# A transformer layer on eight cores: one program block for the first stage, a LayerNorm scaling moved from VectorE to ScalarE, and LayerNorm statistics taken block by block

## The reference, cut to what matters

```python
x = x + layernorm(attn(layernorm(x)))      # low-rank q and kv (rmsnorm inside), rope, 32 heads
x = x + layernorm(ffn(layernorm(x)))       # x @ W_base.T + b_base + top-2 of 8 rank-16 adapters
# layernorm: (x - mean) / sqrt(var + 1e-5) over 4096 columns, no weights
```

## Time and profile before

| | |
|---|---|
| median of 3 runs | 4936.53 us (4935.33 to 4947.84) |
| the profiled execution, its own time | 4936.56 us |
| its span on the slowest core (6) | 4935.0 us |
| spans of all cores | 4914.4 to 4935.0 us |
| PE busy | 3475.6 us (70%) |
| ACT busy | 1290.4 us (26%) |
| DVE busy | 981.7 us (20%) |

### The profile page before, as it was taken

How to read it: one execution, slowest core, us unless ns; L and a number is a source line. 1 busy time by engine, 2 the same in 40 slices (tenths; PEclk the granted TensorE clock), 3 DMA queues, 4 the chain that set the end, 5 groups by cost and what they waited for, 6 DMA issues and landing times. The chain is left out here.

```text
span 4935.0 us, 43733 instructions; the slowest of 8 cores (4914.4 to 4935.0 us)
## 1 busy us (share of the span) xinstructions
PE 3475.6 (70%) x16282; PEld 1368.9 (28%) x16282; DVE 981.7 (20%) x2552; ACT 1290.4 (26%) x1957; POOL 66.7 (1%) x129
## 2 busy tenths in 40 slices
PE   2444358188888888888888888879998038824881
PEld 1222234032232222223222222214443023312330
DVE  2454400511111111111111111100000630033004
ACT  0111100034444444444443444430000230013001
POOL 0000000000000000000000000000000000000000
PEclk9666679588889888888988888889999559966995
DMA  4111131110000000000000000023331326531662
GB/s 103 64 56 69 47 65 26 22 21 2 13 14 15 14 15 14 3 12 14 14 14 14 14 9 6 1 51 66 69 70 35 119 41 114 110 95 37 112 114 79
DMA packets 31375, 219.00 MB, mean 44 GB/s; under 512 B 3888, under 2 KB 4160, under 8 KB 14784
## 3 DMA queue, kind: packets, MB, share of 16 engines
q0 software_dynamic: 17776, 147.97, 16.1%
q1 hardware_dynamic: 13392, 68.24, 3.7%
HBM read 347.37 MB, written 16.78 MB: 74 GB/s over the span
## 5 line engine op out<-in xcount | busy, mean ns | idle before, releaser
L69 ACT ACTIVATE pool<-sPP,pool 128x512 bf16<-128x512 f32 x1024 | 700.0, 687 | 588.7 <-PE sPP L69 588.3
L69 PE MATMUL sPP<-pool 128*128 128x512 bf16 (+1 forms) x2048 | 781.3, 416 | 2.8 <-DVE pool L69 2.8
L69 PE MATMUL PEp<-pool 128*128 128x128 bf16 (+2 forms) x3872 | 595.8, 310 | 147.7 <-DVE pool L69 78.2
L69 PE MATMUL PDq<-pool 128*1 128x512 bf16 (+3 forms) x1792 | 504.8, 344 | 171.6 <-DVE pool L69 117.6
L69 PE MATMUL fP<-pool 128*128 128x512 bf16 (+1 forms) x2176 | 519.7, 397 | 74.7 <-DMA pool<-wbt 37.2
L69 ACT ACT_TABLE_LOAD x92 | 118.0, 1283 | 1531.7 <-PE trP L69 468.6
L69 DVE BATCH_NORM_STATS2 pool<-pool 128x6 f32<-128x512 bf16 (+1 forms) x344 | 208.4, 675 | 1464.6 <-PEq L1681 598.8
L69 PE MATMUL oP<-pool 128*128 128x512 bf16 x2048 | 458.5, 388 | 56.0 <-ACT pool L69 31.1
L69 PE MATMUL PCq<-pool 128*128 128x512 bf16 x1024 | 430.7, 421 | 0.0
L69 PEld LDWEIGHTS PEp<-pool 128*128 128x128 bf16 (+1 forms) x3872 | 301.6, 101 | 445.2 <-issue 292.2
L69 PE MATMUL trP<-pool 128*128 128x128 bf16 (+1 forms) x688 | 80.4, 300 | 417.3 <-DVE pool L69 363.1
(11 more groups left out here) (58 smaller groups left out, 1134.2 us busy)
## 6 DMA issues: line engine op xcount, KB each, us to landing
pool<-wbt POOLq DMA_DIRECT2D x64, 1024.0 KB, 8.6
pool<-xb SPq DMA_DIRECT2D x24, 2048.0 KB, 7.7
pool<-wo POOLq DMA_DIRECT2D x16, 2048.0 KB, 13.2
pool<-wqb POOLq DMA_DIRECT2D x16, 1152.0 KB, 8.9
out<-pool SPq DMA_DIRECT2D x64, 256.0 KB, 2.0
pool<-wqa POOLq DMA_DIRECT2D x4, 3072.0 KB, 21.4
pool<-wkvb POOLq DMA_DIRECT2D x16, 512.0 KB, 10.9
pool<-wkva POOLq DMA_DIRECT2D x1, 4608.0 KB, 32.0
```

The lines of the kernel that those rows point to most:

```text
L69: r = a(*args, **kw)
```

## The change

Stage A1 becomes one block. The load of a tile is issued a step earlier, ln(it) stands ahead of kvchain(it-2) on DVE, and the 4096-column scaling is an ACT instruction. In `a1_kvchain`, `v_rsqrt` gets a wait for that ACT instruction of tile i+2, which reads the shared `col_a`. In stages C and D the statistics of each column block are taken when ACT has copied it out, during the matmuls of the following blocks; `bn_aggr` and one 1/sqrt over all tiles of the stage or group at once (`v_rsqrtN`, the same 15 operations on 128x8 or 128x4) follow the last block. Seven small buffers are added to each of the two stages.

```diff
+    def v_rsqrtN(v, src_ap, out_ap, tx, tt, mg, eps):
...
     def a1_ln(blk, i):
...
-                ln_finish(v, ("ln1sq", i), par)
-                S_.wait(v, tok.get(("lnT_mm_all", i - 2)))
-                v.tensor_scalar(out=ln1_bufs[par][:], in0=x_bufs[par][:],
-                                scalar1=col_a[par][:], scalar2=col_b[par][:],
-                                op0=ALU.mult, op1=ALU.add)
-                tok[("lnapply", i)] = sigV.inc(v.last)
+                tok[("ln1fin", i)] = ln_finish(v, ("ln1sq", i), par)
...
     def a1_kvchain(blk, i):
...
                 S_.wait(v, tok[("kv_ms", i)])
+                if i + 2 < KT:
+                    S_.wait(v, tok[("lnapply", i + 2)])
                 v_rsqrt(v, par, col_c[par][:], 1e-30)
...
-    for it in range(KT + 2):
-        with nc.Block() as blk:
+    with nc.Block() as blk:
+        a1_xload(blk, 0)
+        for it in range(KT + 2):
+            if it + 1 < KT:
+                a1_xload(blk, it + 1)
             if it < KT:
-                a1_xload(blk, it)
+                a1_ln(blk, it)
             if 1 <= it <= KT:
                 a1_kvmm(blk, it - 1)
             if 2 <= it:
                 a1_kvchain(blk, it - 2)
             if it < KT:
-                a1_ln(blk, it)
                 a1_transpose(blk, it)
+
+        @blk.scalar
+        def _(s):
+            s = LastW(s)
+            for i in range(KT):
+                par = i % 2
+                S_.wait(s, tok[("ln1fin", i)])
+                S_.wait(s, tok[("xload", i)])
+                S_.wait(s, tok.get(("lnT_mm_all", i - 2)))
+                s.activation(out=ln1_bufs[par][:], in_=x_bufs[par][:],
+                             func=AF.Identity,
+                             scale=col_a[par][:], bias=col_b[par][:])
...
+                for wv in range(nwA):
+                    S_.wait(s, tok[("lnT_mm", i, wv)])
...
+                    s.copy(out=dst, in_=trP[par][:, 0:nk * 128])
...
@@ stage C, vector @@
+            for b in range(NOB):
+                for ti in range(QT):
+                    S_.wait(v, tok[("o_evac", b, ti)])
+                    v.bn_stats(out=ln3st[:, ti, 6 * b:6 * b + 6],
+                               in_=x1_sb[:, ti, b * OBW:(b + 1) * OBW])
...
+            for ti in range(QT):
+                v.bn_aggr(out=mvv3[:, ti, :], in_=ln3st[:, ti, :])
...
+            v_rsqrtN(v, mvf[:, 1:2 * QT:2], rstd8[:], rs8x[:], rs8t[:],
+                     magic8[:], LN_EPS)
...
+            tok["ln3rdy"] = sigV.inc(v.last)
             for ti in range(QT):
                 par = ti % 2
-                S_.wait(v, tok[("o_evac", NOB - 1, ti)])
-                S_.wait(v, tok.get(("ln3ap", ti - 2)))
-                ln_stats(v, x1_sb[:, ti, :], D, ("ln3s", ti), par)
-                S_.wait(v, tok[("ln3s", ti)])
-                v_rsqrt(v, par, mv[par][:, 1:2], LN_EPS)
-                tok[("ln3sq", ti)] = sigV.inc(v.last)
-                tok[("ln3fin", ti)] = ln_finish(v, ("ln3sq", ti), par)
                 S_.wait(v, tok[("ln3ap", ti)])
                 S_.wait(v, tok[("xr", ti)])
@@ stage C, scalar @@
-                S_.wait(s, tok[("ln3fin", ti)])
+                S_.wait(s, tok["ln3rdy"])
                 S_.wait(s, tok.get(("x1_done", ti - 1)))
                 s.activation(out=t1_buf[:], in_=x1_sb[:, ti, :],
```

More of the change, by code:

```diff
@@ L323, in v_rsqrt @@
                 S_.wait(v, t)
+    def v_rsqrtN(v, src_ap, out_ap, tx, tt, mg, eps):
+        v.tensor_scalar(out=tx, in0=src_ap, scalar1=float(eps),
+                        scalar2=None, op0=ALU.add)
+        t = sigV.inc(v.last)
+        S_.wait(v, t)
+        xi = tx.bitcast(mybir.dt.int32)
+        yi = out_ap.bitcast(mybir.dt.int32)
+        v.tensor_scalar(out=yi, in0=xi, scalar1=1, scalar2=None,
+                        op0=ALU.arith_shift_right)
+        t = sigV.inc(v.last)
+        S_.wait(v, t)
+        v.scalar_tensor_tensor(out=yi, in0=yi, scalar=-1.0,
+                               in1=mg.bitcast(mybir.dt.int32),
+                               op0=ALU.mult, op1=ALU.add)
+        t = sigV.inc(v.last)
+        S_.wait(v, t)
+        for it_ in range(3):
+            v.tensor_tensor(out=tt, in0=out_ap, in1=out_ap, op=ALU.mult)
+            t = sigV.inc(v.last)
+            S_.wait(v, t)
+            v.tensor_tensor(out=tt, in0=tt, in1=tx, op=ALU.mult)
+            t = sigV.inc(v.last)
+            S_.wait(v, t)
+            v.tensor_scalar(out=tt, in0=tt, scalar1=-0.5, scalar2=1.5,
+                            op0=ALU.mult, op1=ALU.add)
+            t = sigV.inc(v.last)
+            S_.wait(v, t)
+            v.tensor_tensor(out=out_ap, in0=out_ap, in1=tt, op=ALU.mult)
+            if it_ < 2:
+                t = sigV.inc(v.last)
+                S_.wait(v, t)
     def ln_stats(v, src, width, key, px):
@@ L420, in a1_transpose @@
         if True:
-            sS0 = sigS.count
             @blk.tensor
@@ L432, in _ @@
                     if wv > 0:
-                        S_.wait(t, (sigS, sS0 + wv))
+                        S_.wait(t, tok[("lnT_evac", i, wv - 1)])
                     for k in range(wv * 16, min(wv * 16 + 16, DK)):
@@ L438, in _ @@
                 tok[("lnT_mm_all", i)] = tok[("lnT_mm", i, nw - 1)]
[L440 to L455, removed]
     def a1_kvmm(blk, i):
@@ L576, in _ @@
                 tok[("kcT_evac", i)] = sigV.inc(v.last)
-    for it in range(KT + 2):
-        with nc.Block() as blk:
+    nwA = (DK + 15) // 16
+    aS0 = sigS.count
+    for i in range(KT):
+        base = aS0 + i * (nwA + 1)
+        tok[("lnapply", i)] = (sigS, base + 1)
+        for wv in range(nwA):
+            tok[("lnT_evac", i, wv)] = (sigS, base + 2 + wv)
+        tok[("lnT_done", i)] = tok[("lnT_evac", i, nwA - 1)]
+    with nc.Block() as blk:
[3 more added lines that the diff above has]
+                a1_xload(blk, it + 1)
             if it < KT:
-                a1_xload(blk, it)
+                a1_ln(blk, it)
             if 1 <= it <= KT:
@@ L586, in build_program @@
             if it < KT:
-                a1_ln(blk, it)
                 a1_transpose(blk, it)
+        @blk.scalar
+        def _(s):
+            s = LastW(s)
+            for i in range(KT):
+                par = i % 2
[5 more added lines that the diff above has]
+                             scale=col_a[par][:], bias=col_b[par][:])
+                tk = sigS.inc(s.last)
+                assert tk == tok[("lnapply", i)]
+                for wv in range(nwA):
+                    S_.wait(s, tok[("lnT_mm", i, wv)])
+                    nk = min(16, DK - wv * 16)
+                    if i < QT:
+                        dst = ln1T_own[:, i, wv * 16 * 128:(wv * 16 + nk) * 128]
+                    else:
+                        dst = ln1T_tmps[par][:, wv * 16 * 128:(wv * 16 + nk) * 128]
+                    s.copy(out=dst, in_=trP[par][:, 0:nk * 128])
+                    tk = sigS.inc(s.last)
+                    assert tk == tok[("lnT_evac", i, wv)]
     psA1.close()
@@ L1198, in build_program @@
     xr_buf = [xr_buf0, xr_buf0]
+    ln3st = calloc(128, [QT, 6 * NOB], F32)
+    mvv3 = calloc(128, [QT, 2], F32)
+    rstd8 = calloc(128, [QT], F32)
+    negmb8 = calloc(128, [QT], F32)
+    rs8x = calloc(128, [QT], F32)
+    rs8t = calloc(128, [QT], F32)
+    magic8 = calloc(128, [QT], F32)
     t1_buf = calloc(128, [D], BF16)
@@ L1244, in _ @@
             v = LastW(v)
+            v.memset(magic8[:].bitcast(mybir.dt.int32), 0x5F3759DF)
+            for b in range(NOB):
[3 more added lines that the diff above has]
+                               in_=x1_sb[:, ti, b * OBW:(b + 1) * OBW])
+            t = sigV.inc(v.last)
+            S_.wait(v, t)
+            for ti in range(QT):
+                v.bn_aggr(out=mvv3[:, ti, :], in_=ln3st[:, ti, :])
+            t = sigV.inc(v.last)
+            S_.wait(v, t)
+            mvf = mvv3.rearrange("p a b -> p (a b)")
+            v_rsqrtN(v, mvf[:, 1:2 * QT:2], rstd8[:], rs8x[:], rs8t[:],
+                     magic8[:], LN_EPS)
+            t = sigV.inc(v.last)
+            S_.wait(v, t)
+            v.tensor_tensor(out=negmb8[:], in0=mvf[:, 0:2 * QT:2],
+                            in1=rstd8[:], op=ALU.mult)
+            t = sigV.inc(v.last)
+            S_.wait(v, t)
+            v.tensor_scalar(out=negmb8[:], in0=negmb8[:], scalar1=-1.0,
+                            scalar2=None, op0=ALU.mult)
+            tok["ln3rdy"] = sigV.inc(v.last)
             for ti in range(QT):
                 par = ti % 2
-                S_.wait(v, tok[("o_evac", NOB - 1, ti)])
-                S_.wait(v, tok.get(("ln3ap", ti - 2)))
-                ln_stats(v, x1_sb[:, ti, :], D, ("ln3s", ti), par)
-                S_.wait(v, tok[("ln3s", ti)])
-                v_rsqrt(v, par, mv[par][:, 1:2], LN_EPS)
-                tok[("ln3sq", ti)] = sigV.inc(v.last)
-                tok[("ln3fin", ti)] = ln_finish(v, ("ln3sq", ti), par)
                 S_.wait(v, tok[("ln3ap", ti)])
@@ L1276, in _ @@
```

(44 more changed lines are left out.)

## The result

The changed kernel is faster: the ratio of its runs to those of before is 0.946, 95% interval 0.942 to 0.949 (10 runs of each; executions in which the cores of one die had a lower clock are left out of it). The profiled execution took 4658.0 us, forecast 4649, against 4936.56; its slowest core, 7, spans 4656.5 us against 4935.0. The difference of the spans, 278.5 us, was forecast as 287.

What follows compares the result with a forecast made beforehand. Stage A1 was taken as bound by a ring where one engine works while the next waits, 33.9 us a step. Savings of 184 (A1) + 39 (C) + 64 (D) = 287 us off 4936.5 give 4649 us, range 4628 to 4690.

Steps and rivals of the forecast that it cites:

- The new ring of A1: Stage A1: DVE's list, with its wait for ACT's scaling, sets a step of 21.8 us instead of 33.9; saves 184 us.
- The lag of PE: Stage A1: PE needs 20.3 us per tile, so it is ready about 1.5 us before it is used.
- ACT's float32 scaling: Stage A1: the 128x4096 scaling on ACT takes 3.80 us like the bfloat16 one, between 3.72 and 4.5.
- The estimate of 3.4 us: Stage A1: scaling time by the skill's 0.833 ns per element; the ring would be 21.4 us, the time 5 us lower.
- The table load: Stage A1: one ACT table load in all; 1.28 us in every ring belongs to the longer-ring rival, chance 0.13.
- the cold-clock rival: Stage A1: TensorE's clock never rises, kv matmuls take 16.6 us, PE's ring 26.3; time 4726 us, chance 0.06.
- The weight-load rival: Stages C and D: DVE statistics hold up POOL's weight loads, at most 77 us; time 4688 to 4726 us, chance 0.05.
- The start: Stage A1: ln(0) ends at 63.8 and kvchain(0)'s copy-out starts at 107.1 us, before 13 steps in the ring.
- Stage C: Statistics hidden under matmuls; the reload of x then sets 12.1 us a tile instead of 18.1; saves 39 us.
- Stage D: Both groups' tails lose their statistics: 9.75 us for each of tiles 2 to 4, 3.0 per first tile; saves 64 us.
- Output stores take 2 us and remain in the chunks' chain: Stage D tails: stores still cost 2 us each in a tile's chain, with tail tiles 14.1 us apart.
- The opposite-side rival: Stage A1: DVE's list closes one ring through all engines, 40.4 us a step; chance 0.02, half of it slower.

Runs made afterwards that it cites:

- E5: Changed kernel, but kvchain in A1 writes its 1/sqrt into its own pair of columns and the new wait is removed; ratio 0.937, span 4644.0 us.
- E3: Changed kernel, but in A1 kvchain(it-2) stands ahead of ln(it) again and the new wait is removed; ratio 0.978, span 4822.8 us.
- E7: Changed kernel, but with a second buffer for the reloaded x in stage C; ratio 0.937, span 4638.2 us.
- E6: Changed kernel, but POOL asks for group 1's first two weight tiles in stage D only after group 0's last add; span 4658.7 us, no ratio.
- E8: Changed kernel with own kvchain columns, late weight loads, two x buffers and a second buffer for ACT's scaled tile in C; ratio 0.928, span 4582.1 us.

## Why the prediction was right

- *The new ring of A1,* 21.8 us, is there, with DVE as its engine and the new wait in it (without the wait, in E5, a step is 2.3 us shorter on six of the cores; with the old order, in E3, the old ring is back). The steps were 21.8 to 22.2. The lag of PE, put at 1.5 us, was 1.4 to 3.5: part of the transposes and matmuls ran at the higher clock level, some waves in 1.05 us instead of 1.87.
- *ACT's float32 scaling,* bounded by 3.72 and 4.5 and taken as 3.80, is 3.80. The Trainium skill (page "ScalarE: Activation LUTs", section "Step-by-step: what each stage is for") gives 0.833 ns per element once the pipe is full, for fp32 and bf16 alike. The traces agree on both: the two types take the same 3.80 us, and ACT's copies of 128 and of 2048 columns, 0.287 and 1.867 us, lie 0.82 ns per column apart. The estimate of 3.4 us that the prediction sets beside the row counts the columns alone. It leaves out what an instruction costs whatever its width; a 128x1 ACTIVATE takes 0.186 us here, which is a part of the 0.4 us left over.
- *The table load* appears once, before the first scaling, and the cold-clock rival did not come: a kv matmul group still takes 9.7 to 10.9 us, and the granted clock of the stage is 0.77, where it was 0.67. The weight-load rival did not come either: PE's waits ahead of `fP` are 71.8 us in all after, 74.7 before.
- *The start.* The forecast had x(0) land as before; its statistics start at 55.83 instead of 54.25, as it takes 10.2 us to land instead of 8.5. That x(1) is now loaded at the same time would explain it; no run tests that. The stage still ends at 422.4 for a forecast 422.0 because errors cancel: the first copy-out is at 107.0 as forecast, since two early waves took 1.06 and 1.05 us, the 13 steps came to 1.8 us more, and what follows them to 1.3 less. The mechanism was right; that the stage was hit to half a microsecond is in part luck.
- *Stage C,* 39.5 us for 39: the reload of x as what is late next was right, and E7 shows it.
- *Stage D,* 54.2 us for 64: this is the mis-sized term. The step "Output stores take 2 us and remain in the chunks' chain" failed for the first pair of group 0. Counted from the last block's copies, the stores come 3 us earlier than before (15.2 us against 18.6), and POOL's loads 7 us later (9.7 against 2.8), because the block now ends behind the statistics and the 1/sqrt; so the stores fell into the loads. That cost 7.1 us there (E6 takes them back), and most of the rest of the 10 us are stores in the tiles of that tail, which took 14.8 to 15.1 us instead of 14.1. The whole sum missed by 8.5 us; small gains elsewhere make up the difference.

The opposite-side rival, one ring through all engines, did not come in the changed kernel; E3 shows such a ring, shorter than the rival's 40.4, at 34.0 us in the step shown, as soon as the order is the old one.

## What to carry to other kernels

Look for the closed ring that sets a step before counting what an engine loses or gains: here the order of two functions on one list, within one block, was worth 12 us a step, while moving 2.4 us of work to an idle engine was worth nothing as long as a shared 128x1 column made the first engine wait for the second. When work on a chain is taken out, name the buffer that closes the next ring; a second buffer for x took 25 us more off stage C (18 off the span). And follow the transfers that a block's end releases: when a chain gets shorter, its first small stores can meet loads that used to be over.

## What the runs showed of the hardware

- Two 256 KB stores issued by SP 5.5 us after two 1 MB loads from POOL were waited for 9.2 us, others 2. In every trace with this overlap, on every core, the first store lands within 0.8 us of the second load, 8.0 to 10.5 us after its own issue; with the loads moved away (E6) it lands 2.0 to 2.5 us after it. Between 4138 and 4160 us the loads' 288 packets carry 2.10 MB and those of four stores, 576, carry 1.05 MB. The Trainium skill (page "DMA: Bandwidth & Descriptors", section "Queues, rings and completion order") says that a DMA engine takes its queues in turn, packet by packet, by which small store packets would advance only as fast as the large ones between them. The counts fit: of the 288 load packets about 167 were left at 4147, and the first store has 144, so that taking turns would end it about when the loads end. No run here separates that from another cause.
- A lone 2 MB load of x in C lands 7.3 us after its issue (8.8 for the last, up to 9.4 in other runs) and paces C at 11.9 us a tile. With two in flight (E8) each takes 8.7 to 11.0 us and one lands every 6.2 to 7.7: overlapping them adds little to the rate, and what the second buffer takes away is the time in which no load is under way.
- The 16 transposes of a wave take from 1.05 to 1.87 us in stage A1 after; before, all 32 waves took 1.86 or 1.87. Two waves of one step after, as windows with the busy time of PE first and the clock third from the end:

```profile
349.40:350.60 1.20, 1.05 (x16) 0.90 (x16) 1.20 (x3) 0.04 (x1) 0.00 (x0) 0.97 0.00 0
352.50:354.50 2.00, 1.87 (x16) 1.63 (x16) 1.90 (x4) 0.00 (x0) 0.00 (x0) 0.50 0.00 0
```

The first is at the higher of TensorE's two levels (2.4 GHz); PE had worked through the kv matmuls until 345.9 and the five transposes until 348.1. The second is at the lower one (1.2 GHz), after PE had stood for 2.10 us behind ACT's copy. Before, at 573.53, PE had stood for 13.24 us, and that wave is at 0.50 too.
